# Later additions on VectorE, more phases of a node chunk in a unit, and runs of one piece, in the planned order of a two-layer graph network

## The chip, the cores and the metric

The kernel runs on one core of one Trainium2 chip. The metric is the device time of one execution in microseconds. Besides the runs that are only timed, one execution was taken with the hardware profiler; its page and its trace are what is read here.

## What is computed

6250 nodes with 96 features and 106,250 edges, sorted by destination. Two graph layers, each followed by a layer norm:

```python
# layer 0
h    = gelu(x @ W_pre + b_pre)
aggr = segment_sum(h[src] * edge_attr, dst)            # 106,250 rows of 96
xx   = x + aggr
x    = layernorm(x + xx + gelu(gelu(xx @ W1 + b1) @ W2 + b2))
# layer 1
deg  = segment_sum(1, dst);  dinv = rsqrt(max(deg, 1))
h    = x @ W_lin.T + b_lin
agg  = segment_sum(h[src] * dinv[src] * dinv[dst], dst)
x    = layernorm(x + relu(agg + x @ W_root.T + b_root))
```

## The kernel before, in words

Layer 0 goes over the edges in 167 **units** of five tiles of 128 edges (the last has one short tile). For each unit GpSimd gathers the rows of h by source (L829, five indirect DMAs; it runs up to eight units ahead of VectorE), VectorE builds a one-hot matrix (`onehot`, L1190) and multiplies the gathered rows by the edge features (`msg`, L1206), and TensorE multiplies the two in float32 (`seg`, L1377), which sums the edges of a **group** (three units, later one) into a window of 128 nodes. VectorE adds the window to `sumT` (L1224).

Layer 1 does not gather. Its sum over edges is a dense product of the node values with a matrix of edge counts. While the units run, VectorE builds one-hots of node pairs (L1281, L1283), TensorE multiplies them (L1408) and ScalarE keeps the **counts** (L915), which SP stores to memory (L685); the last pair belongs to unit 110. The node values come from **chunks** of four node tiles (the last three of two), each through twelve **phases** (`step0`) that pass the work between VectorE, TensorE and ScalarE: w1 and a turn (phase 1, L1452, L1455), w2 (3), the layer norm on VectorE (5, 7), a turn (8, L1464), a copy on ScalarE (9, L942), W_lin and W_root (10), and the splitting into three bfloat16 parts (11, L1083 to L1095). The dense product takes a **span** of 240 nodes times a **piece**, that is one chunk: three matmuls for each node tile (L1437). Consecutive pieces of one span that are summed in one PSUM bank are a **run**; VectorE adds its sum to `sumT` or `upper` (`dense`, L1303, L1301). Three banks take turns, so a run begins only when the sum of the third run before it has been added. SP loads pieces (L696) eight ahead.

After the last unit the pieces that are left are multiplied, chunk 13 goes through its phases, and eleven **sets** of nodes are turned, completed (L1489, L1509), normalized and written out.

The order in which all engines take this work is written by a planner, `schedule()`. It walks over the units. In each it puts the additions that are due, the sums of runs that are waiting (`flush`), the phases of chunks (`steps`, `RATE` phases a unit), and pieces as long as a **credit** of node tiles lasts that grows by `CREDIT` a unit. A new run is begun when `pick` finds a span for which at least `LEAST` node tiles can be taken at once. `built` is unit 110. Every engine takes its own part of this one order strictly in sequence, so what stands behind a waiting instruction waits too.

Of the kernel before, what the change touches and what calls it, by code (L numbers as in the profile page):

```python
# [23 lines left out]
UNITS = BODY_TILES // UT  # L24
TAILS = [P] * (BODY_TILES - UNITS * UT) + [REM]
ALL_UNITS = UNITS + 1
COLS = BODY_TILES + 1
WIDE = 52
GROUPS = WIDE + UNITS - WIDE * GU
# [21 lines left out]
CUTS = len(FINE) - 1  # L51
BATCHES = -(-EARLY_TILES // CT)
XT_AT = (0, 1, 4, 8, CHUNKS)
PHASES = (12, 8)
RATE = (1, 2, 4, 6)
LATER = 1
ZS = 4


# [18 lines left out]
META_AT = 7  # L78
BUILD_AT = 9
BUILD_STEP = 0.65  # L80
CREDIT = (11.0, 16.0)
LEAST = (8, 2)


SETS = (0, 5, 10, 15, 20, 24, 29, 34, 39, 44, 49, 53)
# [28 lines left out]
def last_unit(g):  # L114
    return UNITS if g == GROUPS - 1 else first_unit(g + 1) - 1
# [20 lines left out]
def schedule():  # L136
# [4 lines left out]


    order, pieces, runs = [], [], []
    added = [min(last_unit(g) + LATER, ALL_UNITS) for g in range(GROUPS)]
    steps = {u: [] for u in range(ALL_UNITS)}
    at = 0
    for c in range(CUTS - 1):
        at = max(at, added[needed(c) - 1] + 1)
        rate = RATE[(c >= CUTS - 5) + (c >= CUTS - 3) + (c >= CUTS - 2)]
        for p in range(PHASES[0]):  # L150
            steps[min(at + p // rate, UNITS)].append((p, c))
        at = at + (PHASES[0] - 1) // rate + 1
    known, summed, apart = 0, [0] * SPANS, [None] * SPANS
    stored = [ALL_UNITS] * STORES
    built = BUILD_AT + int((BUILDS - 1) * BUILD_STEP)
    open_run, waiting, credit = [], [], 0.0
# [30 lines left out]
        return best  # L187

    def flush(u):
        while waiting and waiting[0][0] < u:  # L190
            order.append(("dense", waiting.pop(0)[1]))

    def next_piece(u, least):
# [9 lines left out]
    for u in range(ALL_UNITS):  # L203
# [17 lines left out]
        for i in range(slots):  # L221
            for k, (p, c) in enumerate(steps[u]):
                if k * slots // len(steps[u]) == i:
                    order.append(("step0", p, c))
                    if p == PHASES[0] - 1:
                        known = c + 1
            if i < len(pairs):
                order.append(("pair", pairs[i]))
                if pairs[i] == PAIRS - 1 or pairs[i] % GP == GP - 1:
                    stored[pairs[i] // GP] = u + 1  # L230
            if credit >= CT:
                was = len(pieces)
                if open_run or not (waiting and u <= built + 1):
                    next_piece(u, LEAST[u > ALL_UNITS - 12])
                if len(pieces) > was:
                    credit -= tiles_of_cut(pieces[-1][1])
                else:
                    credit = min(credit, 2.0 * CT)
# [1368 lines left out]
```

## Time and the profile before

| | us |
|---|---|
| median of 3 runs | 1655.67 |
| lowest and highest of them | 1640.36, 1659.41 |
| profiled execution | 1638.62 |
| its span, first to last instruction | 1636.8 |
| mean granted TensorE clock | 0.816 of full speed |

The profiled execution lies near the lower end of the runs. Times below are microseconds from the start of its span; 1.8 us lie outside the span.

### The profile page before, as it was taken

The numbers are of one execution on the slowest core, as the hardware profiler recorded it, in microseconds if no ns is written. First come the engines' busy times: TensorE is split into PE (matmuls) and PEld (weight loads), VectorE is DVE, ScalarE is ACT, GpSimd is POOL, SyncE is SP. The second block draws the span as 40 slices with busy tenths as digits, with TensorE's granted clock in tenths as the row PEclk, the third lists the DMA queues.
The fourth block names the chain that finished last, engine by engine and source line by source line (L and its number), as shares of the span: only waits on it lengthen the run. The fifth ranks groups of instructions, "written<-read, shape, count | busy, mean of one in ns | idle before, by whom it ended". The sixth has DMA issues, their size and how long they took to land.

```text
span 1636.8 us, 21570 instructions
## 1 busy us (share of the span) xinstructions
PE 1092.7 (67%) x7839; PEld 911.3 (56%) x7839; DVE 720.9 (44%) x1396; ACT 504.6 (31%) x825; POOL 827.7 (51%) x927
## 2 busy tenths in 40 slices
PE   3274455655555766766668877787876388839897
PEld 2263233333334645655567675677766287738797
DVE  7028455655464465363445545432214133333435
ACT  0121345455453454343345345330000000000105
POOL 7457656655555455454445544454555545554003
PEclk9977767768778768887988988888888598958999
DMA  6432455545455465564666666675656266626653
GB/s 151 113 99 60 147 166 179 180 150 163 134 183 158 128 220 176 173 218 122 199 196 217 201 208 196 191 234 148 198 166 167 62 179 161 190 61 179 161 131 77
DMA packets 192321, 263.64 MB, mean 161 GB/s; under 512 B 70450, under 2 KB 169778, under 8 KB 185234
## 3 DMA queue, kind: packets, MB, share of 16 engines
q1 hardware_dynamic: 164528, 218.27, 43.1%
q0 software_dynamic: 27392, 43.48, 11.3%
q8 instruction: 66, 1.08, 0.3%
q10 hardware_dynamic: 290, 0.45, 0.1%
q14 instruction: 45, 0.37, 0.1%
HBM read 175.09 MB, written 87.00 MB: 160 GB/s over the span
## 4 chain that ended last, share of the span: by engine, by line
PE 48%; another core or an unknown queue 23%; ACT 14%; issue 10%; DVE 4%; DMA 0%; DVEq 0%; SPq 0%; ACTq 0%
PE bank_q L1437 23%; ACT counts_raw L915 12%; PE seg L1377 10%; PE bank_q L1408 9%; PE bank_a L1337 1%; PE bank_q L1509 1%; DVE onehot L1190 1%; DVE hots_raw L1283 1%; PE bank_q L1337 1%; DVE msg L1206 1%; PE seg L1509 0%; PE bank_b L1469 0%; PE bank_b L1337 0%; PE bank_q L1489 0%
## 5 line engine op out<-in xcount | busy, mean ns | idle before, releaser
L829 POOL DMA_INDIRECT gath<-table_h,srcs x791 | 764.4, 966 | 677.5 <-DVE msg L1206 456.6
L915 ACT CAST counts_raw<-bank_q 128x490 bf16<-128x490 f32 x625 | 403.3, 696 | 504.0 <-remote 244.6
L1437 PE MATMUL bank_q<-piece_raw,early_late 128*96 128x240 bf16 (+1 forms) x3735 | 476.0, 283 | 55.5 <-issue 53.0
L1437 PEld LDWEIGHTS bank_q<-piece_raw,early_late 128*96 128x96 bf16 x3735 | 429.5, 134 | 85.9 <-issue 78.8
L1408 PE MATMUL bank_q<-hots_raw 128*128 128x245 bf16 x1250 | 268.0, 313 | 302.1 <-ACT counts_raw L915 230.2
L1408 PEld LDWEIGHTS bank_q<-hots_raw 128*128 128x128 bf16 x1250 | 102.8, 106 | 427.1 <-ACT counts_raw L915 286.8
L1377 PE MATMUL seg<-onehot,msg 128*97 128x128 f32 x1662 | 286.0, 331 | 68.7 <-issue 47.4
L1377 PEld LDWEIGHTS seg<-onehot,msg 128*97 128x97 f32 x1662 | 258.3, 211 | 81.1 <-issue 58.0
L1281 DVE TENSOR_TENSOR hots_raw<-counters,kb 128x1024 bf16<-128x1024 bf16 (+1 forms) x157 | 107.2, 683 | 214.7 <-PE bank_q L1408 160.3
L1283 DVE TENSOR_TENSOR hots_raw<-counters,kb 128x1960 bf16<-128x1960 bf16 (+1 forms) x157 | 182.5, 1163 | 0.0
L1303 DVE TENSOR_TENSOR sumT<-sumT,bank_q 96x240 f32<-96x240 f32 x91 | 36.4, 400 | 249.9 <-remote 132.3
L1190 DVE TENSOR_TENSOR onehot<-counters,rel 128x640 f32<-128x640 f32 x166 | 134.9, 813 | 0.0
L1206 DVE TENSOR_TENSOR msg<-gath,edg 128x480 f32<-128x480 f32 x166 | 107.6, 648 | 48.8 <-ACT gath L900 48.8
L925 ACT ACTIVATE y<-bank_a,b1c 96x512 f32<-96x512 f32 (+2 forms) x14 | 8.8, 629 | 283.3 <-PE bank_a L1452 201.3
L1224 DVE TENSOR_TENSOR sumT<-sumT,seg 97x128 f32 x62 | 17.6, 284 | 159.5 <-remote 136.2
L1301 DVE COPY upper<-bank_q 96x240 f32<-96x240 f32 (+1 forms) x15 | 5.8, 387 | 121.5 <-PE bank_q L1437 67.5
L840 POOL TENSOR_TENSOR gap<-bns 120x5 f32<-120x5 f32 (+1 forms) x11 | 2.2, 200 | 105.3 <-DVE bns L1114 105.2
L808 POOL DMA_INDIRECT gath<-in_x,srcs x40 | 38.4, 959 | 13.1 <-issue 11.9
L942 ACT COPY x2T<-bank_b 97x512 f32<-97x512 f32 (+2 forms) x14 | 7.5, 535 | 106.9 <-remote 53.6
L1337 PE MATMUL bank_b<-w_pre,early_late 97*128 97x96 f32 x50 | 12.4, 426 | 34.4 <-ACT stage L887 19.1
L1337 PE MATMUL bank_a<-w_lin,x2T 97*128 97x96 f32 x98 | 15.9, 312 | 28.6 <-issue 15.9
L1337 PEld LDWEIGHTS bank_a<-w_lin,x2T 97*128 97x128 f32 x98 | 14.9, 231 | 30.6 <-issue 16.1
(170 smaller groups left out, 584.9 us busy)
## 6 DMA issues: line engine op xcount, KB each, us to landing
counts_hbm<-counts_raw SPq DMA_DIRECT2D x53, 1470.0 KB
piece_raw<-counts_hbm SPq DMA_DIRECT2D x260, 240.0 KB
edg<-in_edge SPq DMA_DIRECT2D x166, 240.0 KB
gath<-table_h,srcs POOLq DMA_INDIRECT x791
piece_raw<-counts_hbm SPq DMA_DIRECT2D x50, 120.0 KB
piece_raw<-counts_hbm SPq DMA_DIRECT2D x26, 180.0 KB
counts_raw<-counts_hbm SPq DMA_DIRECT2D x4, 600.0 KB, 6.8
table_h<-stage SPq DMA_DIRECT2D x12, 192.0 KB
```

The costliest lines, as they stand in the source:

```text
L808: pool.indirect_dma_start(gath[:, t, :], None, x, bass.IndirectOffsetOnAxis(ap=srcs[:, t:t + 1], axis=0)).then_inc(s_xrows[t // CT], 16)
L829: pool.indirect_dma_start(gath[0:k, u % GS * UT + j, :], None, table[0], bass.IndirectOffsetOnAxis(ap=srcs[0:k, t:t + 1], axis=0)).then_in ...
L915: act.copy(counts[:, k % 2, :, i * 2 * WD:(i + 1) * 2 * WD].rearrange("p a (w n) -> p w a n", w=2), bank_q[m % 2][:, 0:2 * KC].rearrange(" ...
L1190: dve.tensor_tensor(onehot[:, s], iota_ps[:].unsqueeze(1).to_broadcast([P, UT, WIN]), rel[:, u * UT:(u + 1) * UT].unsqueeze(2).to_broadcas ...
L1206: dve.tensor_tensor(msg[:, s, :, 0:D], gath[:, slot_tiles(u), :], edg[:, u % ES], ALU.mult).then_inc(s_msg, 1)
L1281: dve.tensor_tensor(hot_b(j)[:, 0:n], iota_b.unsqueeze(1).to_broadcast([P, n, P, 2]), blocks.unsqueeze(2).to_broadcast([P, n, P, 2]), ALU. ...
L1283: dve.tensor_tensor(hot_k(j)[:, 0:n], iota_k.unsqueeze(1).to_broadcast([P, n, KC, 2]), keys.unsqueeze(2).to_broadcast([P, n, KC, 2]), ALU. ...
L1303: dve.tensor_tensor(total, total, run_sum, ALU.add).then_inc(s_dense, 1)
L1337: last = pe.matmul(bank[:, t * D:(t + 1) * D], left_T[:, t * P:(t + 1) * P], w[:], start=True, stop=True)
L1377: last = pe.matmul(seg[g % 2][0:D + 1, 0:WIN], msg[0:k, u % MS, j, :], onehot[0:k, u % MS, j, :], start=(u == first_unit(g) and j == 0), s ...
L1408: last = pe.matmul(bank_q[m % 2][:, w * KC:(w + 1) * KC], hot_b(j)[:, i, :, w], hot_k(j)[:, i, :, w], start=True, stop=True)
L1437: mm = pe.matmul(sums(r)[0:D, 0:n], parts[:, FINE[c] + i, part, :], rows, start=(first and runs[r][3] is None and i == 0 and part == 0), s ...
```

## The change

Five things in the planner change, and nothing in the work itself.

- Sums of groups of three units are added on VectorE two units after the group's last unit instead of one (`LATER`); the first phase of a chunk waits for these additions, so chunks begin a unit later.
- After unit 111 and until four units before the end, `flush` holds the sum of a run back for one unit more.
- From chunk 7 on the phases come at 2, 2, 3, 3, 4 and 6 a unit (before 1, 1, 2, 2, 4, 6).
- After unit 110 the credit grows by 13 node tiles a unit instead of 16.
- After unit 111 a run may begin with 4 node tiles (before 8, and 2 in the last units as now).

```diff
-RATE = (1, 2, 4, 6)
-LATER = 1
+RATE, RATE_LAST = 1, (2, 2, 3, 3, 4, 6)
+LATER = (2, 1)
...
-CREDIT = (11.0, 16.0)
-LEAST = (8, 2)
+CREDIT = (11.0, 13.0)
+LEAST = (8, 4, 2)
...
-    added = [min(last_unit(g) + LATER, ALL_UNITS) for g in range(GROUPS)]
+    added = [min(last_unit(g) + LATER[g >= WIDE], ALL_UNITS) for g in range(GROUPS)]
...
-        rate = RATE[(c >= CUTS - 5) + (c >= CUTS - 3) + (c >= CUTS - 2)]
+        rate = RATE if c < CUTS - 7 else RATE_LAST[c - (CUTS - 7)]
...
     def flush(u):
-        while waiting and waiting[0][0] < u:
+
+        while waiting and waiting[0][0] < u - (u > built + 1 and u < UNITS - 4):
             order.append(("dense", waiting.pop(0)[1]))
...
-                    next_piece(u, LEAST[u > ALL_UNITS - 12])
+                    next_piece(u, LEAST[(u > built + 1) + (u > ALL_UNITS - 12)])
```

Node tiles that the planner puts into each stretch of units, counted in the two orders, and the runs they form:

| units | 0-109 | 110-127 | 128-134 | 135-147 | 148-152 | 153-165 | 166 and after | runs |
|---|---|---|---|---|---|---|---|---|
| before | 500 | 277 | 0 | 216 | 0 | 198 | 54 | 129 |
| changed | 500 | 229 | 92 | 168 | 68 | 166 | 22 | 156 |

In the changed order 61 of the 68 runs that begin in units 148 to 165 are of one piece: 43 of 4 node tiles in units 148 to 160, 18 of 2 after that. Before, the runs that begin in these units have two or three pieces and 6 to 10 tiles.

Line numbers of the changed kernel are two higher. TensorE from unit 127 on, before (x36 is three pieces of four node tiles, x5 one unit):

```order
L1377 MATMUL seg<-onehot,msg 97x128 x5
L1337 MATMUL bank_a<-w,y 128x96 x4
L1437 MATMUL bank_q<-piece_raw,early_late 96x240 x36
L1377 MATMUL seg<-onehot,msg 97x128 x25
L1464 MATMUL bank_b<-ident,xr 97x128 x4
L1377 MATMUL seg<-onehot,msg 97x128 x10
L1337 MATMUL bank_a<-w_lin,x2T 128x96 x4
L1469 MATMUL bank_b<-x2T,w_root 96x512
L1377 MATMUL seg<-onehot,msg 97x128 x5
L1437 MATMUL bank_q<-piece_raw,early_late 96x240 x72
```

and in the changed order, from unit 127 on:

```order
L1439 MATMUL bank_q<-piece_raw,early_late 96x240 x36
L1379 MATMUL seg<-onehot,msg 97x128 x5
L1439 MATMUL bank_q<-piece_raw,early_late 96x240 x48
L1379 MATMUL seg<-onehot,msg 97x128 x5
L1466 MATMUL bank_b<-ident,xr 97x128 x4
L1439 MATMUL bank_q<-piece_raw,early_late 96x240 x36
L1379 MATMUL seg<-onehot,msg 97x128 x5
L1339 MATMUL bank_a<-w_lin,x2T 128x96 x4
L1471 MATMUL bank_b<-x2T,w_root 96x512
L1439 MATMUL bank_q<-piece_raw,early_late 96x240 x36
L1379 MATMUL seg<-onehot,msg 97x128 x5
L1439 MATMUL bank_q<-piece_raw,early_late 96x240 x36
```

Three pieces or more now stand between any two units, where eight units followed each other with only the chunk's phases between them.

VectorE in units 154 to 156, where L1303 adds the sum of a run, before:

```order
L1190 TENSOR_TENSOR onehot<-counters,rel 128x640
L1206 TENSOR_TENSOR msg<-gath,edg 128x5x96
L1303 TENSOR_TENSOR sumT<-sumT,bank_q 96x240
L1190 TENSOR_TENSOR onehot<-counters,rel 128x640
L1206 TENSOR_TENSOR msg<-gath,edg 128x5x96
L1303 TENSOR_TENSOR sumT<-sumT,bank_q 96x240 x2
L1190 TENSOR_TENSOR onehot<-counters,rel 128x640
L1206 TENSOR_TENSOR msg<-gath,edg 128x5x96
```

and in the changed order, from unit 155 on:

```order
L1192 TENSOR_TENSOR onehot<-counters,rel 128x640
L1208 TENSOR_TENSOR msg<-gath,edg 128x5x96
L1305 TENSOR_TENSOR sumT<-sumT,bank_q 96x240 x3
L1192 TENSOR_TENSOR onehot<-counters,rel 128x640
L1208 TENSOR_TENSOR msg<-gath,edg 128x5x96
L1305 TENSOR_TENSOR sumT<-sumT,bank_q 96x240 x4
L1192 TENSOR_TENSOR onehot<-counters,rel 128x640
L1208 TENSOR_TENSOR msg<-gath,edg 128x5x96
```

Three or four sums now stand behind each unit's messages, each of one piece, where there were one or two of two pieces each.

## Rows read from the trace of the kernel before

**Rows 1.** The page: busy shares of the span, and the chain that ended last.
```profile
PE 1092.7 (67%) x7839; PEld 911.3 (56%) x7839; DVE 720.9 (44%) x1396; ACT 504.6 (31%) x825; POOL 827.7 (51%) x927
...
PE 48%; another core or an unknown queue 23%; ACT 14%; issue 10%; DVE 4%; DMA 0%; DVEq 0%; SPq 0%; ACTq 0%
```

**Rows 2.** Windows by stage: busy us (count) of each engine, clock, DMA share, GB/s.
```profile
core 0: us, PE busy (x) PEld busy (x) DVE busy (x) ACT busy (x) POOL busy (x), PEclk, DMA share, GB/s
1078.00:1247.70 169.70, 136.41 (x1057) 121.49 (x1056) 43.15 (x98) 12.67 (x19) 86.98 (x92) 0.84 0.62 179
1247.70:1303.90 56.20, 20.10 (x115) 16.45 (x113) 13.34 (x36) 2.30 (x5) 36.87 (x39) 0.67 0.43 113
1303.90:1424.20 120.30, 103.05 (x808) 94.69 (x809) 38.97 (x91) 4.63 (x7) 58.79 (x62) 0.86 0.61 166
1424.20:1469.00 44.80, 17.72 (x90) 14.33 (x89) 13.53 (x38) 4.63 (x7) 27.70 (x29) 0.64 0.37 97
1469.00:1568.70 99.70, 87.60 (x756) 82.39 (x755) 40.27 (x114) 8.07 (x14) 21.14 (x21) 0.92 0.62 161
1568.70:1586.40 17.70, 17.19 (x167) 16.85 (x165) 7.70 (x21) 0.00 (x0) 0.00 (x0) 1.00 0.74 183
```

**Rows 3.** The same windows for L1206 alone: units whose messages were multiplied.
```profile
1078.00:1247.70 169.70, 12.17 (x19) 0.84 0.62 179
...
1303.90:1424.20 120.30, 8.40 (x13) 0.86 0.61 166
...
1469.00:1568.70 99.70, 7.76 (x12) 0.92 0.62 161
```

**Rows 4.** Timeline after the last unit: start us, us, engine, line, what.
```profile
1568.68 6.32 PE L1437 MATMUL bank_q<-piece_raw,early_late 128*96 128x240 bf16 x60
...
1576.88 9.01 PE L1437 MATMUL bank_q<-piece_raw,early_late 128*96 128x240 bf16 x90
...
1583.85 0.40 DVE L1303 TENSOR_TENSOR sumT<-sumT,bank_q 96x240 f32<-96x240 f32 x1 [0.21 <-PE bank_q L1437]
```

**Rows 5.** Timeline of the first stretch without pieces.
```profile
1264.36 0.60 PE L1464 MATMUL bank_b<-ident,xr 128*97 128x128 f32 x4
...
1266.47 2.61 PE L1377 MATMUL seg<-onehot,msg 128*97 128x128 f32 x20 [1.51 <-issue]
...
1284.29 0.58 ACT L942 COPY x2T<-bank_b 97x512 f32<-97x512 f32 x1 [26.14 <-remote]
...
1304.78 0.29 DVE L1224 TENSOR_TENSOR sumT<-sumT,seg 97x128 f32 x1 [35.86 <-remote]
```

**Rows 6.** Gathers of the same stretch, and of the whole span (L829).
```profile
L829 POOL DMA_INDIRECT gath<-table_h,srcs x35: 940/944/1216, 1255.3 to 1298.0; - x35
L829 POOL DMA_INDIRECT gath<-table_h,srcs x791: 897/944/4775, 88.2 to 1506.9; - x198
```

**Rows 7.** Chain in order of time: its two longest steps of unknown release.
```profile
1268.92 35.73 another core or an unknown queue
...
1437.44 27.43 another core or an unknown queue
```

**Rows 8.** A chunk's turn with pieces behind it, from the timeline at 1146 us.
```profile
1146.15 0.60 PE L1464 MATMUL bank_b<-ident,xr 128*97 128x128 f32 x4
1147.14 0.58 ACT L942 COPY x2T<-bank_b 97x512 f32<-97x512 f32 x1 [25.45 <-PE bank_b L1464]
```

**Rows 9.** Waits between 1078 and 1568 us: engine, line, releaser: us, times, longest.
```profile
POOL gath L829 <- DVE msg L1206: 138.5, 24, 12.0
...
PE seg L1377 <- DVE onehot L1190: 12.5, 4, 4.4
```

**Rows 10.** L1224, the addition of a group, over the span: idle time before it.
```profile
  remote: 136.2, 15
```

**Rows 11.** Waits between 500 and 1086 us for the one-hots of the pairs.
```profile
PE bank_q L1408 <- DVE hots_raw L1283: 16.7, 7, 4.9
```

## The prediction

> **What bounds the kernel now.** I read the page first: no engine is busy for more than 67% of the span, and the chain that ended last is half TensorE and a quarter steps whose release the profile doesn't know [rows 1]. So I cut the time after the last pair of counts into stages, where pieces, units and chunks share the engines [rows 2], and counted the units in each by the multiplications of messages [rows 3]. Three stages with pieces, 169.7 + 120.3 + 99.7 = 389.7 us, hold 19 + 13 + 12 = 44 units and, by the order, 277 + 216 + 198 = 691 node tiles. TensorE is busy for 80 to 88% there: it sets the pace. Two stages without pieces, 56.2 + 44.8 = 101.0 us, hold the 12 units between; TensorE is busy for 36 to 40% at a clock of 0.67 and 0.64 [rows 2]. VectorE's messages wait for nothing but their place in the order. After the last unit 54 tiles follow, with nothing beside them, before the turned sets may begin: 17.7 us at full clock.
>
> Inside the stages without pieces the time is not what the work needs. In the first, TensorE's turn of chunk 8 stands at 1264.36, but ScalarE's copy, which waits for it, starts at 1284.29, and VectorE waits 35.86 us for a group's sum whose matmuls stand in the trace long before [rows 5]. These are the chain's two longest unknown steps, 35.7 and 27.4 us [rows 7]. All of it lies in a train of 35 gathers without a pause [rows 6]. The same turn of chunk 7, with pieces queued behind it, was followed by its copy 0.4 us after its end (1147.14 against 1146.15 + 0.60) [rows 8]. I can't tell from this trace whether TensorE is slow there because little is queued or because the gathers run; the forecast uses the pace of the stages with pieces, which holds both.
>
> **The empty units filled.** A node tile is three matmuls; after the last unit, undisturbed, 60 take 6.32 and 90 take 9.01 us, 0.307 us a tile [rows 4]. The stages with pieces then leave (389.7 - 691 x 0.307) / 44 = 4.0 us for a unit, with its share of the chunks' phases and of all stalls. The changed order has 723 tiles in 56 units over the same part: 56 x 4.04 + 723 x 0.307 = 226 + 222 = 448 us, where the span now takes 490.7. That is 42.5 us less.
>
> Its bounds come from the split between unit and tile. If a unit cost only its own ten matmuls, 1.3 us (20 in 2.61) [rows 5], a tile would cost (389.7 - 57) / 691 = 0.48, and the sum 421 us: 70 less. If each of the 12 added units cost the whole train of its five gathers, (1298.0 - 1255.3) / 34 = 1.26 us each, 6.3 a unit [rows 6], the 101 us would become 12 x 6.3 + 32 x 0.307 = 85: 16 less. I take 42.5, the one whose tile price is a measured row.
>
> **The tail.** 54 tiles become 22: 32 x 0.307 = 9.8 us, with nothing beside them [rows 4]. The chain of chunk 13 and the sets behind is untouched and stays late by itself.
>
> **Runs of one piece.** 27 more additions of 0.40 us are 11 us of VectorE, which is busy for 40% or less of the stages [rows 2]: nothing on the path. What can cost is the turn of the three banks: in units 148 to 165, 68 runs begin, 61 of one piece, and each needs the sum of the third run before, for which only two pieces are left as cover, 2.5 us or 1.2. After the last unit even runs of two tiles leave no gap on TensorE, with an addition each 0.62 us [rows 4], but VectorE has no other work there. Between 0 and 68 x 0.40 = 27 us; I take 5, near the tail's row.
>
> **Additions held back.** VectorE sits 136.2 us in front of L1224 for unknown releases [rows 10], and more before L1303. Moving these waits frees VectorE, not TensorE: from 1078 to 1568 us TensorE waited for a one-hot of VectorE for 12.5 us in all [rows 9], and up to unit 110 for the pairs' one-hots, which stand behind the addition, for 16.7 [rows 11]. A gain between 0 and 29 us; a loss if a bank's release comes late: units alternate between two banks, and the addition two units later still stands two units before the bank is needed. I take 0. The chunks' later start is covered by the pairs, which take until unit 110 anyway; only chunk 7 moves past them, by a unit, and its doubled phases return it. Two or three phases a unit put ScalarE's functions between TensorE's pieces of one unit: three pieces, 3.7 us, stand between most dependent phases. SP passes the loads of pieces in the new order, eight ahead as before; DMA at 0.62 has room [rows 2].
>
> **The sum.** 42.5 + 9.8 - 5 = 47 us, so 1638.6 becomes 1591 for an execution like the profiled one (its span and 1.8 us around it). The executions shown lie in two pairs, 1638.6 and 1640.4, 1655.7 and 1659.4; their middle is 1648. As a median I expect 1648 - 47 = **1601**.
>
> **Rivals.** 1. *Gathers don't touch TensorE.* Then the stalls [rows 5] came from the thin queue alone and go entirely: the first bound, 70 + 10 = 80 us, 1568. The Trainium skill's page "SBUF — State Buffer", section "SBUF: two separate sides", says so: on the engines' side only the port pair of VectorE and GpSimd contends, TensorE waits for nobody. For it: the turn of chunk 7 [rows 8]. Against: the stalls end with the train [rows 5, 6].
>
> 2. *The gathers set the pace.* 243 gathers remain at 1078 us [rows 2], 305 us of trains. Filling the empty units lays pieces into trains where TensorE hardly moved. The second bound, 16 + 10, less 5 to 27 for the runs: 0 to 21 us saved, 1627 to 1648. Against it: GpSimd still waits 138.5 us for VectorE in this part [rows 9].
>
> 3. *Slower: VectorE becomes the partner that every piece waits for.* In units 148 to 165 VectorE has three to seven sums a unit in its strict order, between messages and the layer norms of chunks 10 to 12. If a run begins late by p, the loss is 68 p. The gain of 52 is gone at p = 0.77 us, and from p = 1.0 the kernel is over 1% slower; at 1.1 it is 75 us, 1671. A one-hot and messages alone are 1.5 us. Against: TensorE's cover of 2.5 us, and the tail's runs [rows 4].
>
> 4. *The low clock.* If the short groups of matmuls let the granted clock of units 148 to 165 fall from 0.92 to the 0.64 of an empty stage [rows 2], their 234 tiles take 72 / 0.64 - 72 / 0.92 = 34 us more: 1635. The skill's page "TensorE: Matmul & The Clock Gate", section "A second HAM failure mode: psum-queue depth-cycling", describes such a fall when banks are cycled in short groups. The trace speaks against it: cycling three banks with groups of six matmuls kept 1.00 [rows 2, 4].
>
> 5. *It doesn't do what it says.* Excluded for the place of the pieces by the order itself; the pieces could come late from memory, which would leave the time where it is.
>
> **The chances.** The forecast, 1580 to 1622: 0.58; rival 1: 0.12; rival 2: 0.16, a third of it within 1%; rival 3: 0.06; rivals 4 and 5: 0.08, most of it within 1%. About 1% (16 us) is what a measurement of this kernel can tell from no change. So faster 0.83, the same 0.11, slower 0.06. The range from 1562 to 1640 takes in rival 1 and most of rival 2.
>
> **What would show it.** In windows of the changed trace: no stretch of over 20 us between the last pair and the last unit with TensorE under 60% busy, and a granted clock over 0.8 throughout; the chain without steps of 27 or 36 us; 7 us instead of 17 from the last unit's matmuls to the first turned set; ScalarE's copies of chunks 8 and 10 within some 5 us of the turn's end. Right on the additions: less waiting before L1224, with the first 1078 us unchanged within 10. Rival 3 would show as idle TensorE released by L1303's sums from unit 148 on; rival 2 as TensorE stalls that sit in gather trains with pieces queued, and GpSimd no longer waiting for VectorE. The prediction is wrong if units 128 to 152 take over 8.5 us each though pieces stand in them.

## The result: 1.1% slower where the forecast was 3% faster, and the profile after

The kernel before takes 1652.4 us (median of 20 runs, 1636.8 to 1667.5), the changed one 1668.6 us (20 runs, 1651.1 to 1681.3): a ratio of **1.011**, with the 95% interval 1.007 to 1.015. The ratios here are of the runs within 1.5% of each kernel's fastest, so they can differ by a thousandth from the quotient of the medians. The forecast was 1601. On which chip these runs were made isn't recorded; the experiments below ran on four chips. On the first the kernel before takes 1675 us, on the three others 1178 to 1180; on one of those the changed kernel ran too and is faster than before (1164.7 us). That has a section of its own below.

The page of the changed kernel: span, busy shares, the chain that ended last, and two groups of instructions: the gathers, and the one-hots of the pairs.

```profile
span 1664.2 us, 21647 instructions
PE 1084.4 (65%) x7839; PEld 898.5 (54%) x7839; DVE 729.4 (44%) x1423; ACT 504.8 (30%) x825; POOL 829.6 (50%) x927
...
PE 45%; another core or an unknown queue 19%; issue 18%; ACT 13%; DVE 4%; DMA 0%; DVEq 0%; SPq 0%; ACTq 0%
...
L831 POOL DMA_INDIRECT gath<-table_h,srcs x791 | 766.1, 969 | 715.1 <-DVE msg L1208 492.5
...
L1283 DVE TENSOR_TENSOR hots_raw<-counters,kb 128x1024 bf16<-128x1024 bf16 (+1 forms) x157 | 107.3, 684 | 279.8 <-PE bank_q L1410 223.5
```

The shares are those of before [rows 1], and TensorE is no busier. The waits at the additions did go: the same view as [rows 10], of the line that is now L1226, shows

```profile
  PE seg L1379: 26.9, 1
  remote: 16.1, 2
```

where 136.2 us in 15 waits stood. VectorE now waits elsewhere, at places that also need TensorE: before the pairs' one-hots it sits idle for 279.8 us (214.7 before). The windows from the message of unit 110 to that of the last full unit, and from there on:

```profile
1099.00:1560.00 461.00, 345.96 (x2623) 307.56 (x2622) 137.08 (x339) 27.18 (x42) 233.88 (x241) 0.81 0.57 158
1560.00:1599.00 39.00, 31.28 (x248) 29.72 (x246) 23.26 (x68) 5.69 (x9) 0.00 (x0) 0.87 0.51 126
```

The pieces are spread as intended, yet TensorE is busy for 75% (345.96 of 461) with a clock of 0.81. Over the whole of the same part of before, with its stretches without pieces, it was busy for 364.9 of 490.7 us, 74%, at 0.82. So nothing was filled up: the stages with pieces fell from 80 to 88% [rows 2] to the mean. From unit 110's message (1098.8) to the last full unit's (1598.6) it is 499.8 us; before, 477.8. The timeline shows how the stretch has changed. These are some of VectorE's messages (L1208) and its long waits from unit 113 to 120:

```profile
1124.84 0.65 DVE L1208 TENSOR_TENSOR msg<-gath,edg 128x480 f32<-128x480 f32 x1
1127.19 0.64 DVE L1208 TENSOR_TENSOR msg<-gath,edg 128x480 f32<-128x480 f32 x1
1128.81 0.64 DVE L1208 TENSOR_TENSOR msg<-gath,edg 128x480 f32<-128x480 f32 x1
...
1152.54 0.56 DVE L1085 TENSOR_TENSOR stage<-bank_a,by_degs 128x384 f32<-128x384 f32 x1 [22.57 <-PE bank_a L1339]
...
1156.46 0.65 DVE L1208 TENSOR_TENSOR msg<-gath,edg 128x480 f32<-128x480 f32 x1
...
1162.49 0.65 DVE L1208 TENSOR_TENSOR msg<-gath,edg 128x480 f32<-128x480 f32 x1
...
1194.26 0.16 DVE L1303 COPY upper<-bank_q 96x10 f32<-96x10 f32 x1 [31.13 <-PE bank_q L1439]
```

VectorE does five units in 6 us (1156.46 to 1162.49), as many as the ring of messages lets it, then waits 31 us for a bank of TensorE. Five units done at once are 25 gathers that GpSimd may issue without a pause, and it does, from 1157.4 to 1189.0. From 1164 to 1194 TensorE is busy for 8.5 of 30 us, at a clock of 0.50. That is a stall of the kind in [rows 5], but now with pieces queued.

### The profile page after: what moved, and what is told of

Its sections match the earlier page's. It is cut to its first block, busy times and chain, and to the rows that moved or that the text cites. A ratio compares the mean times of both kernels' runs of the same rounds, so it can differ in the third digit from the quotient of the medians.

```text
span 1664.2 us, 21647 instructions
## 1 busy us (share of the span) xinstructions
PE 1084.4 (65%) x7839; PEld 898.5 (54%) x7839; DVE 729.4 (44%) x1423; ACT 504.8 (30%) x825; POOL 829.6 (50%) x927
## 4 chain that ended last, share of the span: by engine, by line
PE 45%; another core or an unknown queue 19%; issue 18%; ACT 13%; DVE 4%; DMA 0%; DVEq 0%; SPq 0%; ACTq 0%
PE bank_q L1439 18%; ACT counts_raw L917 11%; PE bank_q L1410 10%; PE seg L1379 10%; PE bank_a L1339 1%; PE bank_q L1511 1%; PE bank_b L1339 1%; PE bank_q L1339 1%; PE bank_a L1454 1%; DVE hots_raw L1285 1%; PE seg L1511 0%; DMA early_late<-in_xT 0%; PE bank_q L1491 0%; DVE onehot L1192 0%
## 5 line engine op out<-in xcount | busy, mean ns | idle before, releaser
L831 POOL DMA_INDIRECT gath<-table_h,srcs x791 | 766.1, 969 | 715.1 <-DVE msg L1208 492.5
L1439 PEld LDWEIGHTS bank_q<-piece_raw,early_late 128*96 128x96 bf16 x3735 | 419.0, 132 | 127.0 <-issue 114.1
L1379 PE MATMUL seg<-onehot,msg 128*97 128x128 f32 x1662 | 276.2, 324 | 33.9 <-issue 22.1
L1379 PEld LDWEIGHTS seg<-onehot,msg 128*97 128x97 f32 x1662 | 251.2, 206 | 43.2 <-issue 26.7
L1283 DVE TENSOR_TENSOR hots_raw<-counters,kb 128x1024 bf16<-128x1024 bf16 (+1 forms) x157 | 107.3, 684 | 279.8 <-PE bank_q L1410 223.5
L1305 DVE TENSOR_TENSOR sumT<-sumT,bank_q 96x240 f32<-96x240 f32 x114 | 45.6, 400 | 221.0 <-remote 112.2
L1208 DVE TENSOR_TENSOR msg<-gath,edg 128x480 f32<-128x480 f32 x166 | 107.6, 648 | 59.1 <-ACT gath L902 52.4
L1303 DVE COPY upper<-bank_q 96x240 f32<-96x240 f32 (+1 forms) x15 | 5.8, 387 | 110.7 <-PE bank_q L1439 71.6
L1305 DVE TENSOR_TENSOR upper<-upper,bank_q 96x240 f32<-96x240 f32 (+1 forms) x27 | 10.0, 371 | 72.9 <-remote 62.3
L1226 DVE TENSOR_TENSOR sumT<-sumT,seg 97x128 f32 x62 | 17.4, 280 | 47.2 <-PE seg L1379 26.9
L1339 PEld LDWEIGHTS bank_b<-w_pre,early_late 97*128 97x128 f32 x50 | 11.4, 330 | 32.6 <-issue 32.6
```

The costliest lines, as they stand in the source:

```text
L831: pool.indirect_dma_start(gath[0:k, u % GS * UT + j, :], None, table[0], bass.IndirectOffsetOnAxis(ap=srcs[0:k, t:t + 1], axis=0)).then_in ...
L1208: dve.tensor_tensor(msg[:, s, :, 0:D], gath[:, slot_tiles(u), :], edg[:, u % ES], ALU.mult).then_inc(s_msg, 1)
L1283: dve.tensor_tensor(hot_b(j)[:, 0:n], iota_b.unsqueeze(1).to_broadcast([P, n, P, 2]), blocks.unsqueeze(2).to_broadcast([P, n, P, 2]), ALU. ...
L1305: dve.tensor_tensor(total, total, run_sum, ALU.add).then_inc(s_dense, 1)
L1339: last = pe.matmul(bank[:, t * D:(t + 1) * D], left_T[:, t * P:(t + 1) * P], w[:], start=True, stop=True)
L1379: last = pe.matmul(seg[g % 2][0:D + 1, 0:WIN], msg[0:k, u % MS, j, :], onehot[0:k, u % MS, j, :], start=(u == first_unit(g) and j == 0), s ...
```

## The experiments

Three views of the loss stood against each other. **T**: TensorE is held up by long unbroken trains of GpSimd's gathers; VectorE's waits at the additions kept VectorE, and so GpSimd, from running ahead, and the change took these brakes away. **B**: later additions cost by themselves. **R**: gathers don't touch TensorE; the loss comes from the order of the work.

### The parts of the change one by one

Only the groups' additions later:

```diff
-LATER = 1
+LATER = (2, 1)
-    added = [min(last_unit(g) + LATER, ALL_UNITS) for g in range(GROUPS)]
+    added = [min(last_unit(g) + LATER[g >= WIDE], ALL_UNITS) for g in range(GROUPS)]
```

> The kernel before with one part of the change: sums of three-unit groups are added two units late; nothing else is moved. Theory T (trains): TensorE's pace falls the longer GpSimd gathers without a pause, and each wait of VectorE for a TensorE sum was a brake that kept the trains short. Then this part alone costs: the first 1078 us become 10 to 20 us longer, trains get longer than the 8.3 gathers they had on average there, ratio 1.005 to 1.015. Rival R (runs): the loss of the whole change comes from runs of one piece and more sums late in the order. Then this part is worth nothing, ratio 0.997 to 1.003. Rival C (clock): as R.

Measured: 1696.3 us against 1675.3, ratio 1.017 (1.011 to 1.023), a little over T's range. Later additions alone cost at least as much as the whole change. "Nothing else is moved" isn't quite so: chunks begin later, and the planner leaves 70 node tiles instead of 54 for the time after the last unit. By the prediction's 0.307 us a tile that is 4.9 us, and in the profiled execution 84.0 us follow the last full unit's messages, where 81.1 did. That leaves 16 to 18 us, some 1%, for the moved waits.

Only the filling:

```diff
-RATE = (1, 2, 4, 6)
+RATE, RATE_LAST = 1, (2, 2, 3, 3, 4, 6)
...
-CREDIT = (11.0, 16.0)
-LEAST = (8, 2)
+CREDIT = (11.0, 13.0)
+LEAST = (8, 4, 2)
```

> The kernel before with the pieces and phases spread as in the change (phases 2, 2, 3, 3, 4, 6 a unit, credit 13, runs from four node tiles), but sums of groups and of runs stay where they were, so VectorE keeps its brakes. Theory T: the units without pieces are filled and no long trains come in their place: 15 to 45 us less, ratio 0.972 to 0.991. Rival R (runs of one piece and more sums cost): ratio 1.00 to 1.01, with TensorE idle behind the sums of runs from unit 148 on.

Measured: 1667.6 us, 0.996 (0.992 to 1.000). T's number was missed, by half a point. The profiled execution shows where: after the last full unit's messages 65.0 us are left where 81.1 were, so the tail gained 16, and the units from 110 to the last took 492.9 us, not less than the 477.8 of before. Filling the empty units gave nothing there.

The filling and the sums of the spans held back, without the later additions:

```diff
-        while waiting and waiting[0][0] < u:
+        while waiting and waiting[0][0] < u - (u > built + 1 and u < UNITS - 4):
```

> The kernel before with the changed rates, credit and least pieces, and with the spans' sums held back one unit, but the groups' additions where they were. Without pace. Theory T: the held-back sums take away the second brake, so VectorE runs ahead and units 110 to 165 take longer than with the rates alone (0.996 of before): 1.000 to 1.012. Rival: the sums' place costs nothing, 0.990 to 1.000, and all of the change's loss is the later groups' additions.

Measured: 1689.3 us against 1678.5 on the same chip, 1.010 (1.005 to 1.015). Its order has every unit's pieces where the filling alone has them (20 tiles after the last unit, 147 runs, in both); only the sums stand later. So against the filling alone this step costs some 1.4%, and nothing but the place of the sums can be its cause. Each of the two moves of waits costs by itself; together, in the whole change, they cost no more than one.

### The waits put back in another place

If the brakes were what counted, a brake elsewhere must do as well. Gathers for unit u wait until TensorE has begun unit u-8:

```diff
                     pool.wait_ge(s_msg, u - GS + 1)
+                    pool.wait_ge(s_pace, u - 8 + 1)
...
+                    if j == 0 and n > 1:
+                        last.then_inc(s_pace, 1)
```

On the kernel before:

> The kernel before, and GpSimd's gathers for unit u also wait until TensorE has begun unit u-8 (a new semaphore that TensorE raises with the first matmul of each unit), so a burst of VectorE no longer starts a long train. Same work, one more wait. Theory T: the trains of 30 and 35 gathers are gone, few have over 10, TensorE's two steps of 36 and 27 us shrink to under 10, ratio 0.96 to 0.99. Rival N (the stalls are TensorE's own, from thin work, and the trains only fall in with them): the two steps stay and the ratio is 1.00 to 1.02, since gathers come later.

Measured: 1581.8 us, **0.945** (0.939 to 0.950): more than T said. An added wait of an engine took 5.5% off. But the two long steps didn't shrink to under 10 us, as T had it: the chain still has steps of 31.4 and 27.0 us, in two trains of 25 gathers (1225 to 1256 us and 1386 to 1418) that the pace let through in the stretches without pieces. So the gain must have come from the other trains. On the filled kernel:

> The spread pieces and phases of the second kernel of this set together with the paced gathers of the third. Theory T: both gains add, ratio 0.94 to 0.975, and TensorE is over 80% busy from the last pair to the last unit. Rival N: as the second kernel, or slower by the later gathers, ratio 0.98 to 1.01.

Measured: 1561.3 us, 0.934 (0.928 to 0.939). Here TensorE is busy for 82% from unit 110 to the last full unit, and ScalarE's copies of chunks 8 and 10 come 3.3 and 0.6 us after the turn (19.3 and 19.9 before). And on the whole change:

> The changed kernel, whole, and GpSimd's gathers for unit u also wait until TensorE has begun unit u-8. Theory T (the additions' and groups' waits were brakes that kept GpSimd's gathers in short trains, and TensorE is slowed by long trains): with the trains kept short by the wait itself, the change's first and third part cost nothing any more, and it stands beside the kernel before with pace and filled units (0.934): 0.925 to 0.945 of the kernel before. Rival B (later additions cost by themselves, say by groups' banks held longer or by VectorE's bursts): it keeps the loss of 1.7 per cent over that, 0.945 to 0.96.

Measured: 1561.6 us, **0.930** (0.925 to 0.935). With the brake the change's moved additions cost nothing (0.930 with them, 0.934 without), and the filling is worth about a point. B falls for this chip. The group of gathers in that last kernel's page, in the columns of the page's fifth part:

```profile
L833 POOL DMA_INDIRECT gath<-table_h,srcs x791 | 780.3, 986 | 610.7 <-PE seg L1381 293.2
```

GpSimd's idle time now ends mostly by TensorE, 293.2 us, where VectorE's messages had ended 492.5 of 715.1. I counted trains (gathers with less than 0.6 us between one's end and the next's start) after 160 us: in the three kernels with the pace 55 to 135 gathers stand in trains of more than ten, in before, the filled, the held-back, the later-additions and the changed kernel 225, 230, 265, 280 and 305.

### The gathers replaced

```diff
-                    pool.indirect_dma_start(
-                        gath[0:k, u % GS * UT + j, :], None, table[0],
-                        bass.IndirectOffsetOnAxis(ap=srcs[0:k, t:t + 1], axis=0)
+                    pool.dma_start(
+                        gath[0:k, u % GS * UT + j, :], table[0][t % 48 * P:t % 48 * P + k, :]
                     ).then_inc(s_gath[u % GS], 16)
```

> The kernel before with each of the 791 gathers by index replaced by a plain load of as many bytes from 128 consecutive rows of the same table, issued by GpSimd in the same place with the same semaphores. It leaves the gather out: edges get the wrong source rows. Theory T (it is the indirect transfers of GpSimd, a train of them without pause, that slows TensorE): TensorE keeps its pace through the whole of the units, and the time falls to 0.75 to 0.90 of before. Rival S (it is the data written to SBUF or the traffic of the DMA engines, whatever issues it): 0.95 to 1.01. Rival R (TensorE isn't slowed, the units wait for VectorE's order): 0.90 to 1.00.

Measured: 1155.5 us against 1678.5, **0.687** (0.681 to 0.692), below T's range. One of the five runs took 2327.4 us at a clock of 1.00, which nothing here explains; the others lie between 1150 and 1159. The bytes, the packets and the places of the waits are the same, and TensorE's share rises from 67 to 81%:

```profile
PE 940.6 (81%) x7839; PEld 815.0 (70%) x7839; DVE 717.8 (62%) x1396; ACT 498.6 (43%) x825; POOL 480.5 (42%) x927
...
L829 POOL DMA_DIRECT2D gath<-table_h x791 | 417.4, 536 | 539.8 <-DVE msg L1205 526.8
```

R and the rival of mere traffic fall. The test isn't clean, since a plain load also takes GpSimd only 536 ns and not 966; so the cost was measured by itself.

### Trains by themselves

Nothing is computed but this: TensorE makes 30 sets of 24 matmuls (128x128, FP32) that read nothing a transfer writes, and VectorE marks the end of each set with a copy of one column.

```diff
+for i in range(SLOTS):
+    if i % train == 0:
+        pool.wait_ge(s_tick, TICKS * f + i * TICKS // SLOTS)
+    pool.indirect_dma_start(gath[:, i, :], None, x, bass.IndirectOffsetOnAxis(ap=srcs[:, i:i + 1], axis=0)
+                            ).then_inc(s_gath[f], 16)
```

> The disputed cost by itself; nothing of the reference is computed, the output is a copy of x. Eight phases, in each TensorE makes 30 sets of 24 FP32 matmul records (128x128, the size of seg) that read nothing that a transfer writes, and VectorE marks each set's true end. Beside it: phase 1 nothing; 2 to 5 forty gathers in trains of 5, 10, 20 and 40, spread alike over the phase by a clock that ScalarE keeps; 6 forty plain loads of the same size from SP in one train; 7 the train of 40 beside BF16 matmuls; 8 BF16 matmuls alone. Theory T: a set takes 2.6 us at the full clock in phases 1 and 6, and in trains the sets' ends stretch with the train's length: mean set time in phase 5 at least 1.3 times that of phase 2, with a gap of over 15 us between two marks in the train of 40. Rival S: phase 6 is slowed as phase 5. Rival R: all FP32 phases alike within 5 per cent but for the clock.

The windows run from the first mark of a phase to its last: no gathers; forty in trains of 5, 10, 20 and 40; forty plain loads from SP. Columns as in [rows 2].

```profile
8.00:86.00 78.00, 77.72 (x696) 77.53 (x695) 4.77 (x31) 59.63 (x40) 0.00 (x0) 1.00 0.08 18
89.00:167.00 78.00, 77.76 (x697) 77.57 (x695) 4.75 (x30) 58.89 (x40) 35.94 (x39) 1.00 0.12 26
170.00:272.00 102.00, 90.11 (x697) 87.95 (x696) 4.65 (x30) 58.92 (x40) 35.81 (x39) 0.90 0.09 20
275.00:393.00 118.00, 89.26 (x699) 85.60 (x698) 4.80 (x31) 59.13 (x41) 35.96 (x39) 0.84 0.08 17
396.00:521.00 125.00, 86.08 (x696) 83.44 (x696) 4.72 (x31) 58.91 (x41) 35.62 (x39) 0.81 0.07 16
524.00:602.00 78.00, 77.62 (x697) 77.43 (x697) 4.65 (x30) 58.78 (x41) 0.10 (x1) 1.00 0.11 24
```

From mark to mark the phases took 77.7, 77.7, 101.8, 117.3, 124.6 and 77.7 us. The same 40 gathers and the same matmuls: nothing lost in trains of five, 47 us in a train of forty. The marks at the start of the train of forty, and of the first two trains of five, on the timeline:

```profile
401.71 0.16 DVE L92 COPY mark<-bank 128x1 f32<-128x1 f32 x1 [5.63 <-PE bank L124]
445.30 0.16 DVE L92 COPY mark<-bank 128x1 f32<-128x1 f32 x1 [43.44 <-remote]
449.69 0.16 DVE L92 COPY mark<-bank 128x1 f32<-128x1 f32 x1 [4.23 <-remote]
```

```profile
89.08 0.16 DVE L92 COPY mark<-bank 128x1 f32<-128x1 f32 x1 [3.04 <-PE bank L124]
93.47 0.16 DVE L92 COPY mark<-bank 128x1 f32<-128x1 f32 x1 [4.23 <-remote]
94.44 0.16 DVE L92 COPY mark<-bank 128x1 f32<-128x1 f32 x1 [0.81 <-PE bank L124]
97.12 0.16 DVE L92 COPY mark<-bank 128x1 f32<-128x1 f32 x1 [2.52 <-PE bank L124]
```

A set takes 2.68 us alone. In the train of forty one mark stands 43.6 us behind the one before it, 2.5 us after the train's last gather (442.8). TensorE's own rows there:

```profile
402.40 0.27 PE L124 MATMUL bank<-msg 128*128 128x128 f32 x1 [0.25 <-issue]
403.81 0.38 PE L124 MATMUL bank<-msg 128*128 128x128 f32 x2 [1.15 <-issue]
...
432.68 0.37 PE L124 MATMUL bank<-msg 128*128 128x128 f32 x1 [2.43 <-issue]
435.48 0.37 PE L124 MATMUL bank<-msg 128*128 128x128 f32 x1 [2.43 <-issue]
```

For 9.2 us from the train's start they follow each other every 0.11 us, without a gap; then they come ever more seldom, until one stands every 2.8 us, at half the clock; 7 us after the train they are back at full pace. In the other long trains the first gap comes after 8.7 to 10.6 us, 73 to 81 rows, and with BF16 matmuls after 3.4 us, 62 rows. In the trains of five there is no gap at all, and the marks that come 1.7 us late (93.47 after 89.08) are followed by the next one 0.97 us behind. TensorE can't make a set in 0.97 us, and 94.44 is two sets' time after 89.08 to the hundredth: there the matmuls were in time, and only the word of them came late. The same window over the train of forty, on this chip and (second line) on one that doesn't stall:

```profile
394.00:443.00 49.00, 15.82 (x95) 13.92 (x95) 0.32 (x2) 48.20 (x32) 36.91 (x40) 0.62 0.18 40
251.00:300.00 49.00, 49.00 (x441) 49.00 (x441) 3.01 (x19) 48.20 (x32) 35.91 (x39) 1.00 0.19 40
```

The losses, 24.1 us in four trains of ten, 39.6 in two of twenty, 46.9 in one of forty, are 6.0, 19.8 and 46.9 us a train, and the trains last 12.2, 24.7 and 49.7. So a train costs its length less 3 to 6 us. A small part of that is the lower clock after it (0.81 from 450 to 460 us). The BF16 matmuls of phase 7 show the same stall, 91.2 us instead of 38.9. The traffic isn't the cause: the forty plain loads from SP go faster than the gathers, with the DMA engines at 0.43 in their first 16 us, and TensorE's rows have no gap beside them.

With 6 us taken as free, I summed for each profiled execution on this chip and those of the first result what its trains after 160 us have over 6 us each: 404 to 453 us in the five kernels without the pace, with spans of 1637 to 1706, and 314 to 323 in the three with it, with spans of 1566 to 1596. The means differ by 108 us in the sum (428 and 319) and by 94 in the span (1671 and 1577). Within either group the sum doesn't order the spans: one execution differs from the next by as much. So this agrees with T and doesn't prove it.

### The same on other chips

The next four kernels fell on another chip, where the kernel before took 1180.0 us instead of 1675.

> Again the disputed cost by itself, on the same 30 sets of FP32 matmuls; the output is a copy of x and nothing of the reference is computed. Seven phases: 1 no gathers; 2 to 5 forty gathers, GpSimd waiting after every 1, 2, 5 and 10 until they have landed; 6 forty gathers with a memset of GpSimd's own (128x1400) after every 5; 7 all forty in one train. Theory T (TensorE goes on for some 6 us of a train and then stands until it ends, and a short pause lets it catch up: the first such kernel had 77.7, 77.7, 101.8, 117.3 and 124.6 us for no gathers and trains of 5, 10, 20, 40): phases 2 to 4 take 77 to 82 us, phase 5 95 to 105, phase 7 122 to 127, and phase 6 as phase 4 if a pause in the gathers is what counts. Rival (each gather costs TensorE its share, however they are spaced): phases 2 to 7 all over 100.

Measured: 77.7 us in all seven phases, the train of forty among them. Its question, on pauses, wasn't answered.

Two more ran beside it: the filled kernel with a wait for the landing after each unit's gathers, without and with the pace.

> The kernel before with the changed rates, credit and least pieces, and in place of the pace on TensorE a wait of GpSimd after each unit's five gathers until they have landed, so that no train is over five long. Theory T: TensorE loses nearly nothing in trains of 6.2 us, but GpSimd now needs 6.2 us and a landing of 2 to 3 us a unit, 158 units in 1300 to 1450 us, and sets the pace: 0.93 to 1.00 of before. Rival (no bearing of the trains' length): slower than before, 1.00 to 1.08.

> Both waits: rates, credit and least pieces, pace by TensorE's unit u-8, and the wait for the landing after each five gathers. Theory T: the trains of ten that the paced kernel still has (14 to 23 of them in each part) go too, worth up to 6 us each by the experiment on trains; against it the landing after each unit. 0.92 to 0.97 of before, within 3 per cent of the kernel with the landing alone. Rival: as the pace alone or slower by the landings, 0.95 to 1.02.

Measured: 1551.7 and 1550.8 us, 1.314 of before on that chip. Where trains hold nothing up, breaking them is pure loss: GpSimd needs five gathers (6 us) and a landing (it waited 414.6 us in 158 waits, 2.6 each) for each unit. The fourth was the filled kernel with the tighter pace:

> The rates, credit and least pieces with a tighter pace: gathers for unit u wait until TensorE has begun unit u-6. Theory T: fewer trains over five long, but GpSimd idles where TensorE is behind for other reasons: 0.92 to 0.95 of before, against 0.934 with u-8. Rival: GpSimd is now late and its start is on the path, 0.95 to 0.98.

Measured: 1163.6 us, 0.986 (0.984 to 0.987), so nothing can be said of u-6 where it was meant to be tried. Then the changed kernel itself, the filling alone and the changed kernel with the pace ran on a third chip, which took 1178.9 us for the kernel before:

> The changed kernel as it stands, again, beside the kernel before on the same chip. If the chip is of the kind that takes 1180 us for the kernel before: theory T (all of the change's loss is TensorE held up by long trains) gives 0.98 to 1.00, with the gain of the filled units or none, since GpSimd's gathers are on the chain there; rival B (later additions cost by themselves) 1.005 to 1.02. If it is of the kind that takes 1660: 1.005 to 1.018 again under both.

> The rates, credit and least pieces alone, again. On a chip of 1180 us: theory T 0.98 to 0.995, and the changed kernel within 0.5 per cent of it; rival B: the changed kernel at least 1 per cent over it. On a chip of 1660 us: 0.99 to 1.00 again.

> The changed kernel with GpSimd's pace on TensorE's unit u-8, again. On a chip of 1180 us: theory T says the pace has nothing to win there, 0.985 to 1.01, since TensorE isn't held up. On a chip of 1660 us: 0.925 to 0.935 again.

Measured: 1164.7 us, **0.988** (0.986 to 0.990); 1159.7 us, 0.983 (0.980 to 0.986); 1164.5 us, 0.989 (0.986 to 0.991). The pace has nothing to win here, as T says. The change's loss of over 1% doesn't exist here; but the moved additions aren't free: with them the kernel takes 5.0 us more than with the filling alone, though the intervals all but touch, and their order also has nine more runs (156 against 147). So B, or the order, holds for a small part. The page and the gathers' line in the profile of the changed kernel on this chip:

```profile
span 1163.6 us, 21647 instructions
PE 953.0 (82%) x7839; PEld 819.9 (70%) x7839; DVE 732.1 (63%) x1423; ACT 498.8 (43%) x825; POOL 841.3 (72%) x927
...
POOL 44%; PE 30%; issue 15%; ACT 5%; DVE 3%; DMA 2%; DVEq 0%; ACTq 0%; POOLq 0%
```

```profile
L831 POOL DMA_INDIRECT gath<-table_h,srcs x791: 897/944/2158, 66.3 to 1084.1; - x198
its engine sat idle before it (us, times) until:
  issue: 239.6, 786
  DVE msg L1208: 1.5, 5
```

The 791 gathers run in one train from 66.3 to 1084.1 us with nothing between them but 0.3 us of issue, and TensorE beside them is busy for 82%. GpSimd is the head of the chain: 1017.8 / 790 = 1.29 us a gather.

The last two questions, pauses on a chip that stalls, were put twice more, on the third chip and on a fourth:

> Trains and pauses by themselves, TensorE making 30 sets of FP32 matmuls in each of ten phases: 1 no gathers; 2 to 4 forty gathers in trains of 5, 10 and 40 by ScalarE's clock; 5 to 8 GpSimd waits after every 1, 2, 5 and 10 until they have landed; 9 a memset of GpSimd's after every 5; 10 forty plain loads from SP. The output is a copy of x. On a chip of 1180 us: 77.7 us in all ten. On a chip of 1660 us, theory T: phases 1 to 4 77.7, 77.7, 102, 125; phases 5 to 7 under 82, phase 8 95 to 105, phase 9 as phase 7 if only the pause counts, phase 10 77.7; rival (each gather costs its share however spaced): phases 5 to 9 over 100.

> Trains and pauses by themselves, the same kernel of ten phases again. On a chip of 1180 us 77.7 us in all ten. On a chip of 1660 us, theory T (TensorE goes on for some 6 us of a train, then stands until it ends, and catches up in a pause): phases 1 to 4 77.7, 77.7, 102, 125; phases 5 to 7 (landing awaited after 1, 2, 5 gathers) under 82, phase 8 (after 10) 95 to 105, phase 9 (a memset after 5) as phase 7 if only the pause counts, phase 10 (plain loads) 77.7. Rival (each gather costs its share however spaced): phases 5 to 9 over 100.

> The rates, credit and least pieces with a wait for the landing after each unit's five gathers, again. It took 1551 us on the chip of 1180, where GpSimd's gathers and landings set the pace. On a chip of 1660 us, theory T: trains of five cost TensorE nearly nothing, so it takes about as long as on the other chip, 1545 to 1590, 0.925 to 0.95 of before. Rival: gathers cost TensorE their share however spaced, and both waits add up: 1.00 or more.

Both chips were of the fast kind (1178.9 and 1177.6 us for before). All ten phases took 77.7 us on the third chip and on the fourth. On the third, the windows of the trains of 10 and of 40:

```profile
170.00:248.00 78.00, 77.87 (x698) 77.68 (x696) 4.68 (x30) 58.99 (x40) 35.89 (x39) 1.00 0.13 26
251.00:329.00 78.00, 77.91 (x698) 77.72 (x697) 4.64 (x30) 59.04 (x40) 35.91 (x39) 1.00 0.12 26
```

The kernel with landings took 1552.2 us, 1.316. So two questions stay open: how short a pause of GpSimd may be to spare TensorE, and what the whole kernel takes on the chip that stalls when no train is over five long.

## Why the prediction was wrong

**The stall's cause was set aside, and the working rested on that.** The prediction said of the stretches without pieces: "I can't tell from this trace whether TensorE is slow there because little is queued or because the gathers run; the forecast uses the pace of the stages with pieces, which holds both." It doesn't hold both. Trains are as long as VectorE lets them be, and the change altered just that. The trace had the answer nearer than it looked: the stalls ended within 6 us of the train's end [rows 5, 6], while the one row that seemed to acquit the gathers, chunk 7's prompt turn [rows 8], was not set beside its train: one of ten gathers that had begun at 1145.1, 2 us before the copy. In the trains by themselves the first mark, 3 us in, was in time too.

**Filled units, -42.5 us: the step that failed; nothing came.** From unit 110's message to the last full unit's it took 492.9 us with the filling and 499.8 with the change, against 477.8. These are single executions; up to unit 110, where the kernels before, filled and held-back have the same order but for the first phases of chunk 7, they stand at 1077.9, 1100.7 and 1127.2, so no 20 us between two of them mean much. The medians of many runs say the same: the filling gained some 7 us in all on that chip, less than its tail. Four microseconds for a unit was not a price of the unit. It was a mean over stages whose trains had 5 to 15 gathers; in the changed kernel the part after unit 110, all with pieces, holds two trains of 25 and five of 15. What the trains after unit 110 have over 6 us each is 159 us before, 140 with the filling and 163 with the change: the stalls weren't filled, they moved.

**The tail, -9.8 us: right, and larger.** 81.1 us became 65.6 from the last full unit's messages to the end: 11.3 us less between the last unit's matmuls and the first turned set (18.1 to 6.8), and 4.2 less before. On a chip that doesn't stall it is 65.5 with the change; no trace shows the kernel before there.

**Runs of one piece, +5 us: about right.** Between 1400 and 1620 us TensorE waited for an addition in L1305 two times, 3.4 us in all; the runs weren't tried by themselves. Rival 3 didn't happen; the kernel became slower by another mechanism than the one that I priced.

**Additions held back, 0: the second step that failed, a loss where nothing was expected.** "Moving these waits frees VectorE, not TensorE" was right as far as it went, and the bound below, 0, had only a bank's late release as its reason to lose. Freed, VectorE runs up to the next wait, GpSimd's gathers follow it in a train, and the train holds TensorE. Alone the groups' part costs 1.7%, 3 to 5 us of it by more tiles in the tail, and the spans' part 1.4% over the filling; with the pace on GpSimd both cost nothing. Part of the loss lies before unit 110, where both orders hold 500 node tiles: the trains from 160 us to there have 291 us over 6 us each in the changed kernel and 304 with the later additions alone, against 248, 263 and 273 in the three kernels without them. I didn't ask what the freed engine would start.

**The rivals.** Rival 1, that gathers don't touch TensorE, drew on what the Trainium skill's page "SBUF — State Buffer" states in its section "SBUF: two separate sides". That section is on the ports of SBUF. On one chip of this case what rival 1 made of it is false (43.6 us for a set), on three it is true; whether the stall has anything to do with the ports, no run shows. Where gathers do leave TensorE alone, the gain was 14 us and not rival 1's 80, since GpSimd sets the pace there. Rival 2, gathers set the pace and 0 to 21 us are saved, is what the fast chips show: 14 us saved, GpSimd at the head of the chain. It had 0.16. No rival had the case that came, a change of the trains' length.

**What would show it.** Two signs came: less waiting before the groups' additions, and 6.8 us instead of 18.1 to the first turned set. The others didn't. From 1157 to 1190 us TensorE is busy for 13.0 of 33 us at a clock of 0.59. The copies of chunks 8 and 10 start 11.0 and 8.9 us after the turn's end. Unit 110 comes 21 us later than before. Units 128 to 152 take 9.7 us each (before 7.8, with the filling alone 9.4), over the 8.5 that I had named as the sign of being wrong. The chain's unknown steps of 27 and 36 us are gone, the longest after unit 110 being 14.78 us, but one of 88.79 us from 1386.42 on has taken their place, which the view calls issue, since it knows nothing that ScalarE waited for. Of the two signs for rival 2 the trace met one, stalls in gather trains with pieces queued; GpSimd still waited for VectorE, 492.5 us.

**A version that beats both.** On the chip that stalls, the filling with the pace beats both kernels by over 5% (1561.3), with the change's moved additions or without. On a chip that doesn't stall, the filling alone is best (1159.7), and the pace cost the changed kernel nothing that can be measured (1164.5 against 1164.7). Where the chip isn't known, the filled and paced kernel is the one to keep, and the moved additions the part to leave out; with this pace it wasn't run on a chip that doesn't stall, only with the tighter one (0.986, against 0.983 for the filling alone on another chip).

## What to carry to other kernels

A wait that costs its own engine nothing may be what keeps another engine's issue in short pieces. Before you remove one, ask what the freed engine will start, and how long it can run until the next wait stops it. And where a trace shows an engine slow for an unknown reason, measure that reason alone, in a kernel of a few lines, before a pace that contains it goes into a sum. If two runs of the same kernel on two chips differ by a third, look for a behaviour that one of them has and don't average over it.

## What the runs showed of the hardware

On one chip an unbroken train of GpSimd's indirect gathers of 128 rows holds up TensorE: a mark of VectorE's came 43.6 us after the last, where a set takes 2.68. The matmuls read nothing that the gathers write, the DMA engines are busy for 18% in that train, and plain loads of the same size, 40 in a train, leave TensorE alone. TensorE's rows go on at full pace for the first 9 to 11 us of a train (3.4 with BF16 matmuls), then they come ever more seldom, in the train of forty one every 2.8 us, until 2 to 7 us past its end. In all a train costs its length less 3 to 6 us, and in trains of five nothing is lost. On three other chips trains of 10 and of 40 lost nothing, and the kernel before took 1178 to 1180 us instead of 1675. The ratio, 0.70, is near the 0.69 that plain loads in place of the gathers gave on the first chip, so the stall seems to be all of the difference between the chips; that is argued, not shown.

What in that chip does it was not found. That TensorE lacked instructions is a rival that wasn't tried. The trace speaks against it, no more: the packets of the instruction queue that keep step with TensorE come mostly 128 matmul rows apart, and over the train of forty it was 126 rows (394.5 to 455.4 us), so they seem late because TensorE was slow. Every trace here, on all four chips, is of core 0, so whether it is the chip, the core or something that had gone before is open too.

A matmul's row in the trace is no proof that its result is free to use. In the stall in [rows 5] twenty of TensorE's rows end at 1269.1, and the addition that waits for the group starts at 1304.78; in the train of forty the third set's rows end, by their number and pace, near 401.2, and its mark stands at 445.30. Such a wait shows as one for "remote". The waiting engine's own row tells when the result could be used.
